# A causal attention stage: outputs of a head group in one PSUM bank, mask matmuls in quarters of the array, new issue order

## The reference, cut to what matters

```python
qkv = x @ W_attn + b_attn
q, k, v = split_heads(...)                  # 16 heads of 8
q, k = apply_p_rope(q), apply_p_rope(k)
attn = einsum('bhqd,bhkd->bhqk', q, k) / sqrt(8)
attn = softmax(where(causal_mask, attn, min))
y = einsum('bhqk,bhkd->bhqd', attn, v)
y @ W_proj + b_proj                         # then gated and added to x
```

## Time and profile before

| what | value |
|---|---|
| median of the runs | 1144.67 us |
| the profiled execution, first to last instruction (its own time, the span) | 1139.4 us |
| attention: first Exp to the end of the stage | 137.7 to 540.2 us |
| one group of four heads in the steady part | 24.31 to 24.34 us |
| PE busy over the whole span | 952.8 us (84%) |
| DVE busy | 820.3 us (72%) |
| ACT busy | 701.6 us (62%) |
| POOL busy | 456.0 us (40%) |
| granted TensorE clock, mean of the span | 0.903 |

### The profile page before, as it was taken

The page is one execution under the profiler, slowest core; times in us unless marked ns, Lnnn a source line. Parts: engine busy times, 40 slices in busy tenths (PEclk is TensorE's granted clock), DMA queues, the critical chain, the costliest instruction groups (busy, mean ns, idle before and its releaser), DMA issues. The chain is left out here.

```text
span 1139.4 us, 26868 instructions
## 1 busy us (share of the span) xinstructions
PE 952.8 (84%) x9021; PEld 620.4 (54%) x9021; DVE 820.3 (72%) x2061; ACT 701.6 (62%) x1465; POOL 456.0 (40%) x526
## 2 busy tenths in 40 slices
PE   4675699999999999998678899984867769999993
PEld 2342243334333333344455688874655558999991
DVE  5888889999999999965866555556585874644434
ACT  3695277787888777775464566664602656666660
POOL 5807221223321122221277756561200176775441
PEclk9886599999999999999688999997968766999996
DMA  7235202111111100000321332639056233342216
GB/s 211 75 121 183 94 32 74 39 39 40 55 52 46 40 30 30 2 2 1 89 71 52 98 83 73 192 92 298 2 150 169 63 101 95 82 107 72 66 52 228
DMA packets 102430, 96.90 MB, mean 85 GB/s; under 512 B 15181, under 2 KB 85672, under 8 KB 102296
## 3 DMA queue, kind: packets, MB, share of 16 engines
q1 hardware_dynamic: 88120, 75.16, 22.9%
q0 software_dynamic: 8640, 17.84, 4.6%
q10 hardware_dynamic: 5536, 2.18, 0.7%
HBM read 60.05 MB, written 34.82 MB: 83 GB/s over the span
## 5 line engine op out<-in xcount | busy, mean ns | idle before, releaser
L569 DVE TENSOR_REDUCE part<-sps 128x2 f32<-128x1024 f32 (+2 forms) x307 | 327.5, 1114 | 25.6 <-PE sps L557 14.0
L912 ACT ACTIVATE prob<-tpa 128x1024 f32<-128x1024 f32 (+1 forms) x208 | 192.8, 927 | 45.4 <-PE tpa L858 43.6
L744 POOL TENSOR_SCALAR_AFFINE_SELECT prob<-prob 128x512 f32<-128x512 f32 x128 | 80.5, 641 | 306.2 <-ACT prob L912 306.2
L1791 POOL DMA_INDIRECT yk<-yo,place x142 | 144.7, 1019 | 104.1 <-ACT yo L1820 85.5
L1247 POOL DMA_INDIRECT xg<-pair,slot x128 | 127.2, 994 | 91.5 <-DVE slot L1398 53.5
L878 PE MATMUL ops<-prob,vs 128*32 128x512 f32 (+3 forms) x1536 | 157.9, 498 | 0.1
L912 ACT ACTIVATE prob<-tpb 128x512 f32<-128x512 f32 (+1 forms) x224 | 126.8, 566 | 35.2 <-PE tpb L858 35.1
L550 PE MATMUL sps<-qk 48*128 48x512 bf16 (+2 forms) x734 | 133.0, 339 | 12.3 <-DVE part L569 8.3
L1910 PE MATMUL banks<-xT,y 128*128 128x128 f32 x852 | 109.1, 279 | 1.6 <-ACT y L1805 0.7
L1848 DVE COPY place<-xt 128x1 uint32<-128x1 uint32 x142 | 21.7, 153 | 115.7 <-ACT esg L1814 77.9
L1910 PEld LDWEIGHTS banks<-xT,y 128*128 128x128 f32 x852 | 102.8, 195 | 2.8 <-issue 2.0
(11 more groups left out here) (365 smaller groups left out, 1870.9 us busy)
## 6 DMA issues: line engine op xcount, KB each, us to landing
xt<-xg SPq DMA_DIRECT2D x142, 65.0 KB
qk<-term SPq DMA_DIRECT2D x24, 256.0 KB, 2.7
qk<-qk SPq DMA_DIRECT2D x64, 96.0 KB
arena<-kpad SPq DMA_DIRECT2D x6, 1024.0 KB, 12.0
powers<-powr SPq DMA_DIRECT2D x8, 516.0 KB, 5.7
pair<-powers SPq DMA_DIRECT2D x8, 516.0 KB
qk<-qk SPq DMA_DIRECT2D x64, 64.0 KB
pair<-yk SPq DMA_DIRECT2D x8, 512.0 KB, 6.9
```

What stands on the lines that cost most here:

```text
L569: return nc.vector.tensor_reduce(to, src, AX.X, ALU.max, negate=True)
L744: nc.gpsimd.affine_select(out=blk, in_=blk, pattern=[[0, HQ], [1, P]], compare_op=ALU.is_ge, fill=0.0, base=0, channel_multiplier=-1).then ...
L912: nc.scalar.activation(prob[:, at:at + len(units), 0:n], slot_of(t, m)[:, :, 0:n], ACT.Exp, scale=float(HD) ** -0.5).then_inc(exp_done, 1)
L1791: nc.gpsimd.indirect_dma_start(out=d.yk, out_offset=bass.IndirectOffsetOnAxis(ap=place[:, u:u + 1], axis=0), in_=yo[u][:], in_offset=None) ...
```

## The change

It has several parts, all in the attention stage (and in the 13 row score items of the first group, which `front_phase` issues).

1. `vs` gets 41 columns per head in place of 32: the first 512 queries use columns 9 to 40, the second columns 0 to 31, so that the outputs of the first land in rows 0 to 8 of a head's 32 rows and those of the second in rows 9 to 17 of the same bank, in one accumulation. ACT copies `ops` once per group.
2. PE turns this copy once, in one ring place with the maxima of the group two later (`both_item`: one bf16 matmul of the maxima, already split, into the second bank of the place, and four transposes into the first). DVE copies the maxima (64 rows x 128) and then the outputs (128x288) out of PSUM, and takes one reciprocal of 128x32 from SBUF later (`NORM`).
3. The multiplication by the reciprocals moves from DVE to POOL (`normalise`, two of 128x128 per group), and so does the split of the maxima in two bf16 terms (`split_maxima`, two of 128x32).
4. The gate is folded into the projection's weights by POOL (one 128x128 product per batch), and DVE adds a projected tile to x in one instruction in place of two.
5. Each value chunk is issued in two pieces (of 256 or 192 columns, or its two parts), so 20 pieces in place of 10 chunks.
6. The mask matmuls are 64 rows by 64 output partitions (`tile_position` (lo, 64u)) in place of 64 by 128.
7. `Sides` lets the two halves of the array take turns over item borders.
8. `PERIOD`, `LATE` and `BEFORE` are new. One more small DMA loads `identb` in `front_phase`.

```diff
-    for at, x in enumerate(heads):
-        for s in range(2):
-            lo = 64 * s
-            ins = nc.tensor.matmul(out[:, s, at * wd:(at + 1) * wd], qk[lo:lo + KR, 0, x, i * P:(i + 1) * P],
+    per = len(heads) * (1 + diag)
+    for s, piece in sides(per, per):
+        at, mask = divmod(piece, 1 + diag)
+        x, lo, end = heads[at], 64 * s, (at + 1) * wd
+        if not mask:
+            ins = nc.tensor.matmul(out[:, s, at * wd:end], qk[lo:lo + KR, 0, x, i * P:(i + 1) * P],
                                    qk[lo:lo + KR, 1, x, c0:c0 + wd], start=True, stop=not diag,
                                    skip_group_check=True, tile_position=(lo, 0))
-        for u in range(2 * diag):
-
-            for s in range(2):
-                lo = 64 * s
-                ins = nc.tensor.matmul(out[:, s, (at + 1) * wd - P + 64 * u:(at + 1) * wd], w.half[lo:lo + 64, 0, u, :],
-                                       w.half[lo:lo + 64, 1, u, 64 * u:], start=False, stop=u == 1,
-                                       skip_group_check=True, tile_position=(lo, 0))
+        for u in range(2 * mask):
+
+            ins = nc.tensor.matmul(out[64 * u:64 * u + 64, s, end - P + 64 * u:end], w.half[lo:lo + 64, 0, u, 64 * u:64 * u + 64],
+                                   w.half[lo:lo + 64, 1, u, 64 * u:], start=False, stop=True,
+                                   skip_group_check=True, tile_position=(lo, 64 * u))
...
+    [], [(S, 1, 7), (V, -1, 18)], [(S, 1, 8), (V, -1, 19), (S, 1, 9)], [], [(S, 1, 10), (V, 0, 0)], [(V, 0, 1)], [(S, 2, 0)],
+    [(S, 1, 11)], [(S, 1, 12)], [(V, 0, 2), (V, 0, 3)], [(S, 1, 13)], [(S, 1, 14)], [(V, 0, 4), (V, 0, 5), (S, 1, 15)], [],
+    [(S, 1, 16), (V, 0, 6), (V, 0, 7)], [(S, 1, 17)], [(S, 1, 18), (V, 0, 8), (V, 0, 9)], [(S, 1, 19)],
+    [(V, 0, 10), (LEAST, 1, 0), (V, 0, 11), (S, 2, 1)], [(S, 2, 2)], [(V, 0, 12)], [(S, 2, 3)], [(V, 0, 13), (BOTH, 1, 0)],
+    [], [(NORM, -1, 0), (S, 2, 4), (V, 0, 14), (V, 0, 15)], [(S, 2, 5)], [(S, 2, 6), (V, 0, 16), (V, 0, 17)],
...
+class Sides:
+    def __init__(self):
+        self.last = 1
+    def __call__(self, *counts):
+        left, at = list(counts), [0, 0]
+        while any(left):
+            s = 1 - self.last if left[1 - self.last] else self.last
+            yield s, at[s]
+            left[s], at[s], self.last = left[s] - 1, at[s] + 1, s
...
+                def split_maxima(t):
+                    pool.wait_ge(part_done, t + 1)
+                    p = part[t % 2][:].rearrange("p h k -> p (h k)")
+                    nc.gpsimd.tensor_copy(split[:, 0, :], p).then_inc(hi_split, 1)
+                    pool.wait_ge(hi_split, t + 1)
+                    nc.gpsimd.tensor_tensor(split[:, 1, :], p, split[:, 0, :], ALU.subtract).then_inc(max_split, 1)
...
+                def both_item(t):
+                    pe.wait_ge(max_split, t + 1)
+                    after(pe, o_out, t - 1)
                     out = acquire()
-                    for x in range(4):
-                        ins = nc.tensor.transpose(out[:, 0, x * P:(x + 1) * P], osb[half][:, x * P:(x + 1) * P], w.ident[:])
-                    filled(ins)
+                    ins = nc.tensor.matmul(out[0:2 * HQ * TPB, 1, 0:P], split[:].rearrange("p r k -> p (r k)"), w.identb[:],
+                                           start=True, stop=True)
+                    filled(turned_outputs(out) if t >= 2 else ins)
...
+                    o0, v0 = q0 - half * ST, 0 if half else VW - 32
+                    for u, (s, x) in enumerate(UNITS):
+                        h = 2 * s + x
+                        ins = nc.tensor.matmul(ops[32 * h:32 * h + 32, o0:o0 + n], vs[t % 2][:, j, h, v0:v0 + 32],
+                                               prob[:, PBUF[c] * HQ + u, col:col + n], start=c == 0 and piece == 0,
+                                               stop=c == NCH - 1, skip_group_check=True, tile_position=(0, 32 * h))
+                    if piece == 1:
+                        ins.then_inc(pv_done, 1)
```

More of the change, by code:

```diff
@@ L536, with row_scores @@
 NS = len(SITEMS)
-MAXT, O0, O1 = "max", "o0", "o1"
+BOTH, OUT, NORM, LEAST = "both", "out", "norm", "least"
 AHEAD = 13
-def row_scores(nc, w, t, n, out):
+def row_scores(nc, w, t, n, out, sides):
     i, c0, wd, heads = SITEMS[n]
@@ L592 @@
+    (NQUAD, 4): [(NORM, NQUAD - 1, 0)], (NQUAD, 5): [(TURN, 6, 0)], (NQUAD, 6): [(TURN, 7, 0)], (NQUAD, 7): [(PROJ, 6, 0)],
+    (NQUAD, 8): [(PROJ, 7, 0)],
 }
+VW = 32 + HD + 1
 FIRST = AHEAD
-BEFORE = [(S, 0, n) for n in range(FIRST, NS)] + [(S, 1, n) for step in PERIOD for k, q, n in step if k == S and q == 2]
-BEFORE.insert(NS - FIRST + 2, (MAXT, 0, 0))
 def behind(t, m):
-    its = [(k, t + q, n) for k, q, n in PERIOD[m] if t + q < NQUAD and (t + q >= 0 if k in (V, O0, O1) else t + q > 0)]
+    its = []
+    for k, q, n in PERIOD[m]:
+        q += t
+        if 0 <= q < NQUAD and not (k == S and q == 0 and n < FIRST) and not (k == NORM and q >= NQUAD - 2) and not (t < 0 and k in (V, NORM)):
+            its.append((k, q, n))
@@ L602, in behind @@
     return its + LATE.get((t, m), [])
-MAX_AT, O_AT, TURN_AT = {}, {}, {}
+BEFORE = [it for t in (-2, -1) for m in range(NTI) for it in behind(t, m)]
+RING = (S, BOTH, OUT, TURN, PROJ)
+FREE_AT, OUT_AT = {}, {}
 _n = 0
 for _it in BEFORE + [it for t in range(NQUAD + 1) for m in range(NTI) for it in behind(t, m)]:
-    _n += _it[0] != V
-    if _it[0] == MAXT:
-        MAX_AT[_it[1]] = _n
-    elif _it[0] in (O0, O1):
-        O_AT[_it[1], _it[2]] = _n
-    elif _it[0] == TURN:
-        TURN_AT[_it[1]] = _n
+    _n += _it[0] in RING
+    FREE_AT[_it] = _n
+    if _it[0] == BOTH and _it[1] >= 2:
+        OUT_AT[_it[1] - 2] = _n
+    elif _it[0] == OUT:
+        OUT_AT[_it[1]] = _n
@@ L787, in _ @@
             def _(pe):
-                used = [0]
+                used, sides = [0], Sides()
                 def acquire():
@@ L853, in scores @@
                     after(pe, exp_done, prev + 1)
[L854 to L860 removed]
+                    parts = [[(bank, x, part) for bank, (c, u) in enumerate(TITEMS[m]) for sd, x in UNITS[u:u + 1] if sd == side
+                              for part in CHUNKS[c][1]] for side in range(2)]
@@ new lines, in scores @@
+                    for s, piece in sides(len(parts[0]), len(parts[1])):
+                        (bank, x, (j, q0, n, col)), lo = parts[s][piece], 64 * s
+                        ins = nc.tensor.matmul(slot_of(t, m)[:, bank, col:col + n], qk[t % 4][lo:lo + KR + 2, 1, x, j * P:(j + 1) * P],
+                                               qk[t % 4][lo:lo + KR + 2, 0, x, q0:q0 + n], start=True, stop=True,
+                                               skip_group_check=True, tile_position=(lo, 0))
@@ L954, in turn, with reciprocals @@
+                def reciprocals(t):
+                    dve.wait_ge(s_free, OUT_AT[t])
+                    nc.vector.reciprocal(rec[:].rearrange("p x h u -> p (x h u)"),
+                                         raw[:].rearrange("p x h u e -> p (x h u) e")[:, :, HD]).then_inc(rec_done, 1)
                 def turn(s):
@@ L980, in ring @@
                             project(t)
-                        elif kind != V:
-                            o_item(t, n)
+                        elif kind == NORM:
+                            reciprocals(t)
+                        elif kind == LEAST:
+                            least(t)
+                        elif kind == OUT:
+                            outputs(t, ready())
                 ring(BEFORE)
```

206 lines of the change are left out of this document (104 added, 102 removed).

## The result

After takes **1195.15 us** in the median (four runs, 1190.53 to 1211.67), before in the same comparison 1144.81 (1143.68 to 1146.15): a ratio of 1.042 with an interval of 1.039 to 1.046. Slower was forecast, but by 17.8 us and not by 50; the time lies far outside the range. Three runs on record (1211.67 here, 1197.92 in experiment 2, 1201.76 in experiment 6) are slow ones, and every ratio is of the other, fast runs alone.

A forecast was written before the change was run, and what follows sets the result against it. PE and DVE were taken to bound the attention group together. PE's added work made a group 1.2 us longer; 15 x 1.2 + 1.0 + 0.6 - 1.8 = +17.8 on 1144.7 gave 1162.5 us, range 1124 to 1174.

The forecast's parts named there:

- the sign: Whole kernel: slower by over 0.2% was given a chance of 0.66, faster 0.29, within 0.2% 0.05.
- The price of a change: PE in a group: each change of the array's division idles it 0.095 to 0.10 us; 31 more changes, +2.95 us.
- the 0.43: Masks on PE: quarters run side by side, 64 columns less in line at 16 places, -0.43 us per group.
- The sentence on the Trainium skill: Changing tiling mode drains the TensorE, 64x128 and 64x64 are different modes, so the quarter masks pay.
- The steady group: Attention group of four heads: PE's work 25.1 us plus 0.4 of waits, 25.5 us in all, +1.2.
- the weights behind the added changes: PE in a group: weights loaded after the added changes of division, +0.4 us.
- DVE's term: DVE per group: drops 1.36 us, gains a copy of 0.45 and a reciprocal of 0.2; net -0.7, to 22.1.
- the maxima's way: DVE's write to the last DMA: 3.7 us, just covered by 3.7 to 4.1 of PE steps; otherwise up to 0.4 a group.
- The granted clock should stay 1.00 in the stage.: Attention stage: PE's granted clock stays 1.00; were it to fall, nothing of the forecast would hold.
- The last group: Last attention group: no row scores, but six projections, a moved turn and the pieces, +0.6 us.
- The end: Last exponential to the stage's last product: 8.0 us in place of 9.8, so -1.8.
- the start: Ahead of the first group: maxima behind one more row score, three after group 0's last; +1.0 us.

The follow-up runs named there:

- experiment 2: Kernel after with SP issuing group 3's operand load ahead of the maxima of group 1: 1185.66 us, ratio 1.033.
- experiment 6: Kernel after with the item `(S, 2, 0)` put back from step 6 to step 18, no load moved: 1187.68 us, ratio 1.042.
- run 5: Kernel before with quarter masks, and in items with a diagonal and two heads all scores ahead of all masks: 1157.69 us, ratio 1.012.
- run 1: Kernel after with the masks wide again, 64 rows by 128 columns: 1149.18 us, ratio 1.005.
- run 4: Kernel after with wide masks and group 3's load ahead of group 1's maxima: 1141.01 us, ratio 0.997.
- run 3: Kernel before with nothing changed but the masks in quarters: 1165.9 us, ratio 1.020.
- run 7: Kernel after measured once more, unchanged: 1190.43 us, ratio 1.039.
- run 5's second kernel: Kernel after with group 3's load ahead of group 1's maxima, and in items of two heads all scores ahead of all masks: 1160.45 us, ratio 1.013.
- run 8: Kernel of run 4 with projections 4 and 5 moved out of the last group to the end: 1137.14 us, ratio 0.993.
- run 9: Maxima's item `(BOTH, 1, 0)` earlier: at the end of step 21 in run 4's kernel, 1138.61 us; at the start of step 22 in run 8's, 1134.20 us.

## Why the prediction was right about the sign and wrong about the size

**The price of a change: right.** "Each change of the division costs 0.095 to 0.10": the spacings show 0.10 ahead of the quarters, and taking eight changes away gave 0.68 and 0.91 us (run 5), 0.085 and 0.114 each. All quarters together are 25.87 - 23.57 = 2.30 us; with the 0.43 that their side by side saves that is 2.73 for 29 changes, 0.094 each (0.101 by PE's busy time, 25.50 less 23.00). The sentence on the Trainium skill (TensorEngine Tiling (Array Packing), Key Properties) stands as well: a change to 64x64 drains the array like the three others. That the same page counts 64x64 as four independent tiles is borne out as well (four quarters are fed in 0.05 to 0.06 us, four wide masks in 0.08), but it is worth only the 0.43.

**The steady group: nearly right.** Forecast 25.5, measured 25.86 to 25.88. The 0.03 us more behind each set of masks (0.18 in place of 0.15) is not new: the sum had 0.4 for the weights behind the added changes. By the prediction's own way of counting, the group's idle 0.36 and 0.17 for its one shown wait leave some 0.5 of waits and 25.3 of work (an estimate), each 0.1 to 0.2 above the forecast. DVE's term was too good: "a reciprocal from SBUF, 0.2 (bounds 0.15 to 0.3)" measured 0.354, outside its bounds; 32 elements from SBUF cost 0.10 more than the 16 from PSUM of the earlier trace rows, so more elements weighed more than the nearer memory. DVE's busy time fell by 0.2, not 0.7; but with wide masks it fell by 0.6 to 0.7 (22.20 in run 1, 22.14 in run 4), so most of the difference comes with the quarters and not with the reciprocal, and why is open. PE idles only 0.36 of the group, so DVE's term had little to do with its length.

**The step that failed: the new order of the items was costed by its counts, not by what each item needs.** The prediction weighed the maxima's way, "one step later", but passed over the row scores that moved from step 19 to step 6. Of a step that is moved, its operands must be asked after: group 3's come from a load that SP issues behind group 1's maxima (transfers of the kind in the earlier trace rows), and the item reached PE 8.2 us too soon. Runs 2 and 6 take the wait away from both sides. Runs 1 and 4 differ by it alone, with wide masks, and there it is 8 us of time (1.005 to 0.997), more than all that was lost. With quarters it is less plain: the ratio goes from 1.042 to 1.033 in run 2 and stays 1.042 in run 6, where the steady group is 0.3 us longer (4.5 in fifteen) and the clock differs from run to run.

**The second failure: "The granted clock should stay 1.00 in the stage."** It was named as the condition of everything and then given no chance and no price. In the first profile group 0 takes 33.0 against some 26.6 (group 0 of run 3, same masks, clock up earlier), and falls add some 2.3 us in group 1 and 1.4 in group 4: about 10 us, more than the wait. In run 7 the two groups take 86.2, where two steady ones take 51.8. The rise after the start, by the granted clock of each profile: 144.2 to 148.7 us in before and the eight variants with wide masks or with the old order; with quarters and the new order 150.9 (run 5's second kernel), 152.5 (run 6), 160.4 (run 2), 161.8 (after) and 227.7 (run 7). The stretches on either side of the rise for after, and the one ahead of it for run 7:

```profile
93.60:161.80 68.20, 50.72 (x444) 17.91 (x436) 49.10 (x52) 26.51 (x49) 29.42 (x40) 0.50 0.30 106
161.80:182.30 20.50, 16.23 (x210) 6.17 (x210) 14.04 (x15) 11.91 (x19) 4.21 (x8) 1.00 0.14 43
```

```profile
91.20:227.70 136.50, 115.82 (x934) 38.20 (x934) 84.62 (x92) 55.86 (x89) 40.05 (x59) 0.50 0.20 72
```

In these profiles it is late only where both parts of the change are there, and by very different amounts in the same kernel. In the 20 us from 140 on PE shows 19.94 us busy at 0.50 in after, 19.69 at 0.85 in run 3. Why the clock rises later was not settled. It was tried by the item's place and by fewer changes, and each brought the rise forward by some 9 us against its neighbour; with one profile of each, that is a hint.

**The last group: mis-sized.** "+0.6" was 3.9. Six projections stand there in place of four. DVE has time in this group (8.3 us busy of 28), so the step went over them, but PE has none (27.0 of 28.0), and run 8 shows 1.08 us for each projection moved.

**The end and the start: wrong, small.** The end was to be 1.8 us shorter and is 1.3 longer, 0.4 in run 7. From the last exponential's end to the last product 11.0 us pass where 8.0 were forecast. The transposes of the turned outputs take 1.15 us in place of 0.65 and those ahead of the projections 1.16, each at the lower clock, which came down at 578.2 after PE had waited 1.3 us for POOL's masks and 0.7 for the copy; and from the end of the last copy to that of the last product 3.2 pass in place of 2.2. The start was to cost 1.0 and cost 2.5; run 6, with one item less ahead of the maxima, had 3.3, so the item is not it. Run 3 had 2.3 with the old order, and the profiles of all variants lie between 0.4 and 3.3, so a single profile says little here; what it is stayed open.

**The maxima's way: right that it is at the edge.** "Just covered" behind quarters. In the steady group of after PE waits 0.2 us for the rows, in the faster one of run 4 0.6 to 0.7 per group, and run 9 shows that an earlier item turns it into another wait. What the term of "up to 0.4 a group" left out is that single waits are far longer (1.2 ahead of group 4 in after, up to 2.3 in run 8), and that the falls of the clock stand behind those.

**Where the 50 us went**, then, in the first profile: quarter masks in steady groups about 2.3 us each, less about 0.7 that the new order gives back (some 23 us for fifteen groups, where 18 were forecast); one wait of 8.2; some 10 of late or fallen clock; and 3.9 in the last group. Of the 32 us by which the forecast missed, 16.6 stand in groups 0 and 1.

## What to carry to other kernels

A narrower tile of the array pays only if a whole run of work is done in it: count the changes of the division, price each at about 0.10 us (0.085 to 0.12 here), and put matmuls of one division together before making any of them smaller. When a hand-written order is changed, go through every moved item and ask for its first execution, not for a steady one: which load feeds it, and on which queue, behind what. And where PE is busy all the time, a forecast must carry a term for the granted clock: the same kernel spread over 16 us (1186.66 to 1202.91) without its slowest run, and a wait of 1 to 2 us can stand ahead of a stretch at half the clock that costs more than the wait.

## What the hardware showed that was not expected

The granted clock falls from 2.4 to 1.2 GHz in the midst of the stage, mostly for stretches in which PE is busy without a break. In run 8, whose program is that of run 4 up to the last group (run 4's profile has no fall before the stage's end), two of three such stretches, and PE's waits ahead of them:

```profile
191.90:198.80 6.90, 6.90 (x67) 2.76 (x65) 3.67 (x4) 4.09 (x7) 1.27 (x2) 0.51 0.22 81
243.10:250.00 6.90, 6.90 (x66) 2.77 (x64) 3.83 (x4) 4.05 (x7) 1.27 (x2) 0.51 0.24 85
```

```profile
190.43 0.39 PE L921 MATMUL tpb<-qk 50*128 50x512 bf16 x1 [2.34 <-DMA qk<-mrow]
241.80 0.39 PE L921 MATMUL tpb<-qk 50*128 50x512 bf16 x1 [1.85 <-DMA qk<-mrow]
```

The third fall (294.3 to 301.2) stands behind a wait of 1.56. A group with a fall in it takes 26.5 where run 4 has 23.6. Each time the load of another group's operands moves 81 to 86 GB/s in the fall, but SP issues that load right behind the rows for which PE waited.

It is so in every profile of this case. Between the start's rise and the last group they show eleven falls. Nine begin within 2.4 us of the end of a wait for `qk<-mrow` of 1.18 to 2.34 us, or in it, the two others in the long wait for the load of group 3 (after at 182.3, run 1 at 172.1). The three kernels with the old order have neither a wait of 1 us nor a fall from group 1 to group 13. But waits as long also pass without a fall (1.72 at 236.3 us in run 4, 1.56 at 462.4 in run 8), so the wait stands ahead of the fall and does not settle it; no run here makes such a wait on purpose, and that it is the cause is not shown. The waits are long where a transfer of the rows lands late: up to 3.5 us after its issue ahead of 190.4 in run 8, and up to 3.0 ahead of 250.6 in run 2, where most take 1.7. What delays it was not tried.

The times of after against the mean granted clock of each run:

```
us       1190.53  1191.87  1198.43  1211.67     (run 7: 1186.66  1187.28  1193.58  1202.91)
clock      0.884    0.885    0.881    0.868              0.885    0.887    0.877    0.872
```

The longer runs are those with the lower clock, and seven of the eight spread over 16 us, where before has 2.5 in the first comparison and 6.3 in that of run 7. Its steady group is the same to 0.02 us in both profiles.
